# Embedding stage of a one-block vision transformer: loads, scales and all four engine queues in a new order

## The reference

```python
xn = x * rsqrt(mean(x * x, -1) + 1e-6)                       # per patch
scale = 127.0 / clip(max(abs(xn), -1), 1e-5)
xq = clip(round(xn * scale), -128, 127) / scale
ws = 1.0 / clip(mean(abs(w)), 1e-5)
wq = clip(round(w * ws), -1, 1) / ws
h = concatenate([cls, xq @ wq.T], 1) + pos
# attention on layernorm(h)
num = exp(q_rot @ k_rot.T * dh ** -0.5)
den = sum(exp(q @ k.T * dh ** -0.5), -1)                     # without rotation, without mask
h = h + where(causal, num / den, 0) @ v @ Wout + bout
h = h + expert_attention(layernorm(h))
```

## Time and profile before

| what | before |
|---|---|
| median of 3 runs | 259.35 us (258.7 to 259.77) |
| the profiled execution | 258.43 us, span 256.6 us |
| busy in the span | PE 219.7, DVE 181.8, ACT 101.5, POOL 71.3 us |
| instructions | PE 2047, DVE 316, ACT 200, POOL 69 |
| mean granted clock of TensorE | 0.96 |

### The profile page before, as it was taken

The page is one execution under the profiler, slowest core; times in us unless marked ns, Lnnn a source line. Parts: engine busy times, 40 slices in busy tenths (PEclk is TensorE's granted clock), DMA queues, the critical chain, the costliest instruction groups (busy, mean ns, idle before and its releaser), DMA issues.

```text
span 256.6 us, 5086 instructions
## 1 busy us (share of the span) xinstructions
PE 219.7 (86%) x2047; PEld 194.0 (76%) x2047; DVE 181.8 (71%) x316; ACT 101.5 (40%) x200; POOL 71.3 (28%) x69
## 2 busy tenths in 40 slices
PE   0317475999987787999999999999999999999995
PEld 0206374999966555999777788787899999999994
DVE  1598798865379977584244564856679997979982
ACT  3567543885677312657534016425520211120000
POOL 0103648900035020100051555595666000000000
PEclk9999757799999997999999999999999999999999
DMA  7993000000002000000061200704702452461102
GB/s 242 295 411 125 0 1 3 1 0 3 0 3 87 3 3 0 1 3 0 0 187 72 82 3 1 245 3 127 228 3 52 168 155 77 142 213 47 51 0 96
DMA packets 7037, 20.08 MB, mean 78 GB/s; under 512 B 1027, under 2 KB 1606, under 8 KB 6758
## 3 DMA queue, kind: packets, MB, share of 16 engines
q1 hardware_dynamic: 7014, 19.76, 23.7%
HBM read 19.07 MB, written 0.68 MB: 77 GB/s over the span
## 4 chain that ended last, share of the span: by engine, by line
PE 58%; DVE 26%; issue 7%; DMA 3%; ACT 2%; POOL 1%; SPq 1%; DVEq 0%
PE ps L263 15%; PE ps L264 14%; PE ps L265 14%; DVE gx L1073 7%; DVE xhat L807 4%; PE ps L1373 3%; DMA vrow<-vectors 3%; DVE rden L905 2%; PE ps L1248 2%; PE ps L1403 2%; DVE oelo L1047 2%; DVE stat L796 2%; PE ps L1205 2%; DVE en L888 1%; PE ps L1121 1%
## 5 line engine op out<-in xcount | busy, mean ns | idle before, releaser
L1011 DVE COPY_PREDICATED v<-onehot,ps 128x512 f32<-128x512 uint8 (+3 forms) x40 | 26.2, 660 | 24.1 <-PE ps L265 23.9
L1073 DVE TENSOR_TENSOR gx<-maskb,oT 128x1184 fp32r<-128x1184 bf16 x31 | 42.3, 1408 | 0.6 <-PE ps L265 0.5
L263 PE MATMUL ps<-gx,oelo 128*128 128x296 f32 x124 | 37.8, 305 | 0.6 <-DVE gx L1073 0.6
L265 PE MATMUL ps<-gx,oehi 128*128 128x296 f32 x124 | 37.2, 300 | 0.0
L264 PE MATMUL ps<-gx,oehi 128*128 128x296 f32 x124 | 37.0, 298 | 0.0
L263 PE MATMUL ps<-vehi,x2lo 128*128 128x512 f32 (+3 forms) x90 | 35.1, 390 | 0.0
L264 PE MATMUL ps<-velo,x2hi 128*128 128x512 f32 (+3 forms) x90 | 33.3, 370 | 0.0
L265 PE MATMUL ps<-vehi,x2hi 128*128 128x512 f32 (+3 forms) x90 | 33.1, 368 | 0.0
L446 POOL TENSOR_TENSOR velo<-veraw,vehi 128x1024 fp32r<-128x1024 f32 x8 | 19.2, 2404 | 49.2 <-ACT vehi L626 49.1
L263 PEld LDWEIGHTS ps<-gx,oelo 128*128 128x128 f32 x124 | 23.3, 188 | 1.8 <-issue 1.3
L264 PEld LDWEIGHTS ps<-gx,oehi 128*128 128x128 f32 x124 | 23.4, 189 | 0.0
(11 more groups left out here) (162 smaller groups left out, 521.1 us busy)
## 6 DMA issues: line engine op xcount, KB each, us to landing
maskb<-mask_rows SPq DMA_DIRECT2D x32, 148.0 KB, 3.7
veraw<-value_w SPq DMA_DIRECT2D x8, 512.0 KB, 3.9
oeraw<-output_w SPq DMA_DIRECT2D x8, 512.0 KB, 3.6
xp<-x_rows SPq DMA_DIRECT2D x6, 336.0 KB, 6.8
wqraw<-w_qkv SPq DMA_DIRECT2D x1, 1280.0 KB, 11.3
w2raw<-w_qkgate SPq DMA_DIRECT2D x1, 1088.0 KB, 13.3
tw<-tok_weight SPq DMA_DIRECT2D x1, 768.0 KB, 5.0
out<-yo SPq DMA_DIRECT2D x4, 148.0 KB, 1.9
```

The source lines that it names most:

```text
L263: pe.matmul(o, llo, rhi, start=start, stop=False)
L265: return pe.matmul(o, lhi, rhi, start=False, stop=stop)
L1011: dve.copy_predicated(v2[0:m, t, h0:h1], bcast(onehot[0:m, t, h0:h1, e], 2, DH2), ps[0:m, JBANK[n], 0:(h1 - h0) * DH2].rearrange("p (a b) ...
L1073: dve.tensor_tensor(gx[:, k % NGR].rearrange("p a b t -> p a (b t)"), bcast(maskb[:, w % NMR, k % MEU], 1, 2), oT[:, c % 2].bitcast(F32), ...
```

## The change

- **Loads (SP).** The order was x0, weight, x1, x2, constants, vectors, x3, x4, x5. It becomes x0, the identity part of the constants, x1, weight, x2, x3, the other constants, vectors, x4, x5; then as before.
- **Scales per group.** `msq` and its power go to GpSimd, group by group; `quant_scales` takes a list of groups ([0], [1], [2], [3], [4, 5]), multiplies and clamps in one step, and `dqs` is made once for all groups.
- **qT.** All six copies out of PSUM are on ScalarE, and `qT` has four buffers and not two.
- **Queues.** Groups 0 and 1 are quantised before the ternary weight is made; TensorE's start follows a written list, `START`. Four projection jobs stand in it.
- **PSUM banks of the projections** are given out in another order, so that jobs 2 to 5 don't wait for the last `x1_lo`.
- **GpSimd.** `gate_sel` is made early. `qkv_lo(g)` waits until `xhat` of group g is written. The bias additions to `h` come before `w2_lo`, and wait for the last `x1_lo`. The four `w2_lo` wait for the attention's `den_ps` 1, 1, 2 and 3. `ve_lo(0)` waits for the third `x2_lo`, `ve_lo(1)` for the last.
- `w2raw` lies in another part of SBUF, which lives until the end of the attention.

```diff
@@ block.sync
-            sp.dma_start(xp[:, 0, :], x[0]).then_inc(x_in[0], 16)
+            x_load(0)
+            sp.dma_start(cst[:, 0:P], consts[:, 0:P]).then_inc(ident_in, 16)
+            x_load(1)
             sp.dma_start(tw[:], tokw).then_inc(tokw_in, 16)
-            for g in range(1, GI):
-                sp.dma_start(xp[:, g, :], x[g]).then_inc(x_in[g], 16)
-            sp.dma_start(cst[:], consts).then_inc(const_in, 16)
+            x_load(2)
+            x_load(3)
+            sp.dma_start(cst[:, P:], consts[:, P:]).then_inc(const_in, 16)
             sp.dma_start(vrow[:], vecs).then_inc(vec_in, 16)
-            for g in range(GI, G):
-                sp.dma_start(xp[:, g, :], x[g]).then_inc(x_in[g], 16)
+            x_load(4)
+            x_load(5)
@@ banks and TensorE's start
-        PJB = [6, 7, 4, 5] + [0, 1, 2, 3] + [4, 5, 6, 7] + [0, 1, 2, 3] + [4, 5, 6, 7] + [4, 5, 6, 7]
+        PJB = [6, 7, 0, 1] + [2, 3, 4, 5] + [6, 7, 0, 1] + [2, 3, 4, 5] + [6, 7, 0, 1] + [6, 7, 4, 5]
+        START = [("turn", 0), ("turn", 1), ("total", 0), ("bias", 0), ("turn", 2), ("embed", 0), ("turn", 3), ("embed", 1),
+                 ("turn", 4), ("embed", 2), ("turn", 5), ("x", 0), ("embed", 3), ("x", 1), ("embed", 4), ("x", 2),
+                 ("embed", 5), ("x", 3), ("job", 0), ("x", 4), ("job", 1), ("x", 5), ("job", 2), ("job", 3)]
@@ block.gpsimd
-            for b in range(2):
-                pool.wait_ge(sm["msq_ready"], b + 1)
-                s_ = slice(GI * b, GI * b + GI)
-                pool.tensor_tensor(rrms[:, s_], msq[:, s_], half_neg[0:R, :], ALU.pow).then_inc(sm["rrms_ready"], 1)
+            for g in range(G):
+                pool.wait_ge(sm["sq_done"], g + 1)
+                s_ = slice(g, g + 1)
+                pool.tensor_scalar(msq[:, s_], ssq[:, s_], 1.0 / DIN, 1e-6, ALU.mult, ALU.add).then_inc(sm["msq_ready"], 1)
+                pool.wait_ge(sm["msq_ready"], g + 1)
+                pool.tensor_tensor(rrms[:, s_], msq[:, s_], half_neg[0:R, 0:1], ALU.pow).then_inc(sm["rrms_ready"], 1)
+            pool.wait_ge(const_in, 16)
+            pool.tensor_copy(gate_sel[:], bcast(cols("hsel", NH2 * NE), 2, DH2)).then_inc(sm["pool_setup"], 1)
...
-            for g in range(G):
-                pool.wait_ge(sm["lnv_ready"], g + 1)
-                pool.tensor_tensor(rstd[:, 0, g:g + 1], ...)
-                if g < 5:
-                    qkv_lo(g)
+            rstd_of(0, 0)
+            rstd_of(0, 1)
+            for g in range(G - 1):
+                pool.wait_ge(sm["xhat_ready"], g + 1 if g + 2 < G else G)
+                qkv_lo(g)
+                if g + 2 < G:
+                    rstd_of(0, g + 2)
+            pool.wait_ge(sm["x1lo_ready"], G)
+            for g in range(G):
+                pool.tensor_tensor(h[:, g], h[:, g], biasb[:, 1], ALU.add).then_inc(sm["h0b_ready"], 1)
             for n in range(4):
+                pool.wait_ge(sm["den_ps"], max(n - 1, 0) + 1)
                 w2_lo(n)
-            for g in range(G):
-                pool.wait_ge(sm["xhat_ready"], g + 1)
-                pool.tensor_tensor(h[:, g], h[:, g], biasb[:, 1], ALU.add).then_inc(sm["h0b_ready"], 1)
-            for e in range(NVR):
-                ve_lo(e)
+            for g in range(GI):
+                rstd_of(1, g)
+            pool.wait_ge(sm["x2lo_ready"], GI)
+            ve_lo(0)
+            for g in range(GI, G):
+                rstd_of(1, g)
+            pool.wait_ge(sm["x2lo_ready"], G)
+            ve_lo(1)
@@ block.scalar, the start
+            square(0)
+            round_up(0)
+            square(1)
+            quantised_T(0)
+            round_up(1)
+            square(2)
+            square(3)
+            quantised_T(1)
+            square(4)
             act.wait_ge(sm["tern_pre"], 1)
             act.activation(tern[:], tw[:], ACT.Copy, bias=-ROUND).then_inc(sm["tern_ready"], 1)
+            round_up(2)
+            square(5)
+            bias_rows()
+            quantised_T(2)
+            round_up(3)
+            round_up(4)
+            quantised_T(3)
+            round_up(5)
+            wq_hi(0)
+            quantised_T(4)
+            wq_hi(1)
+            quantised_T(5)
+            x1_hi(0)
...
@@ block.vector, the start
+            absmax(0)
+            dve.wait_ge(ident_in, 16)
+            dve.tensor_copy(ident_bf[:], cols("ident")).then_inc(sm["ident_ready"], 1)
+            quant_scales([0])
+            absmax(1)
+            quantised(0)
+            quant_scales([1])
+            dve.wait_ge(tokw_in, 16)
+            dve.tensor_reduce(small[:, 0:1], tw[:], AX, ALU.add, apply_absolute_value=True).then_inc(sm["wabs"], 1)
+            quantised(1)
+            dve.wait_ge(sm["tot_ps"], 1)
...
+            absmax(2)
+            quant_scales([2])
+            absmax(3)
+            quant_scales([3])
+            quantised(2)
...
+            absmax(4)
+            absmax(5)
+            quant_scales([4, 5])
+            dve.tensor_scalar(dqs[:], amc[:], small[0:R, 3:4], None, ALU.mult).then_inc(sm["dqs_ready"], 1)
+            quantised(3)
             embed(0)
-            quantised(3)
+            quantised(4)
             embed(1)
+            quantised(5)
             ln_apply(0, 0)
-            quantised(4)
             embed(2)
             ln_apply(0, 1)
             x1_lo(0)
-            quantised(5)
```

181 lines of the change are left out of this document (75 added, 106 removed).

## The result

| what | before | after |
|---|---|---|
| median, measured together | 259.56 us (258.7 to 260.23) | 248.5 us (247.98 to 249.89) |
| ratio, 95% interval | | 0.960 (0.957 to 0.964) |
| the profiled execution | 258.43 us, span 256.6 | 248.44 us, span 246.6 |
| first matmul of the scores | 69.91 us | 59.07 us |
| first residual addition | 90.66 us | 79.79 us |

A forecast was written before the change was run, and what follows sets the result against it. It took VectorE's chain to bound the kernel, with 6.7 us of held layer norm applications in the embedding. Its terms, -5.8 (job 2 earlier), -1.15 (clock) and -0.1 (attention), made -7.05 from 259.35: 252.3 us, range 250.4 to 255.8.

The forecast's parts named there:

- E: Rival, embedding: every application from the second on is held by wqlo and the power, 261.9 us; chance 0.04.
- F: Rival, projections: rope or ScalarE's reads hold them and hide the gain, only 1 us left, 258.3 us; chance 0.05.
- The clock's term: Start of the projections: TensorE at 2.4 GHz gives back 1.65 us, job 8's wait takes 0.5, net 1.15.
- The attention: Moved w2lo and velo change the holds on mask multiplies: -0.4 to +0.2 us, taken as -0.1.
- A: Main case, embedding to attention: the sum of the terms, -7.05 us, 252.3 us; chance 0.42.
- C: Rival, attention: a pair of w2lo holds the mask multiply for both, 254.4 us; chance 0.18.
- B: Rival, start of the projections: the clock is low again there, 253.4 us; chance 0.18.
- job 2 at 39.6: End of the embedding: TensorE begins the dense projections at 39.6 and not 45.4, 5.8 us earlier.
- The front: Embedding up to embed(0): new small GpSimd steps and waits put embed(0) at 23.95, 1.1 us later than before.
- The rounds: Embedding, one group to the next: 2.1 us on VectorE, 2.1 to 2.3 with TensorE at 1.2 GHz.
- The tail: Embedding's end: embed(5) at 35.3, then TensorE's x3, job 0, x4, job 1, x5; x1_lo(5) ends at 40.4.
- rival D: Embedding: the clock is high there too, VectorE alone paces it, job 2 at 38.2, 250.9 us; chance 0.13.

The follow-up runs named there:

- e3: The kernel before with useless matmuls in TensorE's idle stretches between 26 and 45 us, to keep the clock high; ratio 0.997 (0.993 to 1.001).
- e2: The changed kernel with GpSimd's order of before, all else as changed; 255.35 us, ratio 0.987.
- e8: The changed kernel with the four w2lo still in the attention, but behind the masks of a batch; 246.61 us, ratio 0.952.
- e6: The changed kernel with the four w2lo put behind the last small power, beside the last layer norm application; 252.25 us, ratio 0.972.
- e15: The changed kernel with the transposes of groups 3, 4 and 5 ahead of all four projection jobs, second run; 251.44 us, ratio 0.971.
- e11: The changed kernel with the banks of the projection jobs given out as in the kernel before; 249.99 us, ratio 0.962.
- e14: The kernel before with GpSimd's new order, and VectorE's quantised for group 5 moved ahead of the second application; 249.67 us, ratio 0.967.
- e5: The kernel before with GpSimd's new order alone, run again for another profile; 248.8 to 252.7 us, no interval.
- e1: The kernel before with GpSimd's new order alone, first run; 249.3 us, ratio 0.962.
- e9: The kernel before with GpSimd's new order, and useless matmuls on TensorE before the fifth and sixth groups' transposes; 252.73 us, ratio 0.970.
- e7: The changed kernel with the four w2lo released earlier, when VectorE has finished the third set's rotation and idles; 247.15 us, ratio 0.954.

## Why the prediction was wrong

**Right.** The sign, and the mechanism of the largest term: the three holds are gone, and the `wqlo` between two applications meets the embed (of which only the first instruction reads PSUM). E and F fell with it: no application above 0.42 us, and TensorE busy without a hole in the 3.4 us behind the start of job 2 and still from 44 to 60 (16.0 of 16 us). The clock's term was right: the projections are 23.26 us long from job 2 to the scores (59.07 - 35.81) against 24.53 before (69.91 - 45.38), 1.27 us less where I had 1.65 - 0.5 = 1.15. In e3, where job 8 waits for nothing, they are 22.98 (68.39 - 45.41): the clock gives 1.55, and job 8's wait takes 0.26 and not 0.5. The attention: forecast -0.1, measured 20.72 against 20.75. The mask multiply took 1.91 (forecast 1.8 in A, 3 in C), so a pair of `w2lo` holds it for one of them only, and C fell; B fell by the clock of 1.00 at job 2.

**Wrong: job 2 at 39.6.** It came at 35.81, 3.79 us ahead of that. The step that failed is the working of the embedding, from the front to the last low part of x1: x1_lo(5) ended at 36.86 and not at 40.4, 3.54 us, in three pieces; the last 0.25 is that job 2 begins 1.05 us ahead of that end and not 0.8.
1. *The front, 1.07 us.* "A `tensor_scalar` of one column on GpSimd [...] I take 0.4", and 0.65 for the power. They took 0.19 and 0.56 for the two groups on the path: 0.30 less each time. Half of my bound from nothing to 0.86 was too much for an operation on one column. The weight's sum began at 10.07 and not 10.55, `tern` ended 0.7 earlier, and the steps behind it ran closer together by another 0.4.
2. *The rounds, 1.36 us.* "A round on VectorE is 1.27 + 0.41 + 0.40 = 2.1 us; with TensorE at 1.2 GHz [...] 2.1 to 2.3". Embed(5) was forecast 11.35 us behind embed(0) and came 9.99 behind it (32.87 - 22.88). Some 0.8 us of it is the addition of durations. Of two instructions in a row the next starts up to 0.1 us ahead of the end that its predecessor's row gives: the application at 30.34 lasts 0.41, and the next instruction starts at 30.67. 2.08 added up is 1.90 from start to start. The other 0.57 is what I allowed TensorE at 1.2 GHz between the first application and embed(3) (28.45 to 31.1 for 2.08 of VectorE's work). The clock had risen by then: that group's product took 0.82. And at 1.2 GHz the allowance would have been too much: e2 has one round of 2.11 and the next at 1.90. A round of 1.90, from 37.19 to 39.09, stood in the trace that I predicted from.
3. *The tail, 1.11 us.* From embed(5) to the end of x1_lo(5) I had 5.1 us, by TensorE at 1.2 GHz in turn x3, job 0, x4, job 1, x5; it took 3.99. Here TensorE does set the pace. In the trace of e8, which has the same embedding, the clock stood at 0.63 from 32 to 36 us, embed(0) was 0.24 us earlier and x1_lo(5) ended 0.67 later: by that pair of traces some 0.9 of the 1.1 is clock.

So rival D, a high clock through the embedding, came true from 28 us on, with the 0.13 that I gave it, but explains only the last piece and a part of the second; D itself said 38.2 for job 2, because it inherited the other errors. My argument against it, "at 2.4 GHz TensorE has gaps there", was true of the gaps (0.85 and 0.83 us ahead of two transposes) and false of the clock here: it stayed at 1.00 across them. That was in part luck. In e8 and e6, with two gaps of 0.83 us in the same places, it fell (0.63 and 0.65 from 32 to 36 us); in e15, where a gap of 1.49 us follows, it fell to 0.82.

**The rest of the difference.** 3.79 us of job 2 and 0.12 of the projections make 3.9 at the scores; the median came out 3.8 below the forecast. Between the two profiled executions it is 2.9, since 0.9 us was lost behind the residual addition, which the forecast had at nothing.

**Where the 10.84 us at the scores come from.** Undone one at a time in the changed kernel: GpSimd's order 6.7 (e2), jobs in TensorE's gaps 2.3 (e15), banks 0.95 (e11). These add up to 9.9, if they may be added; the 0.9 left would be the front's, which was not undone alone. Each comes from one pair of traces, and kernels with this same front have embed(0) anywhere from 22.56 to 22.98, so a few tenths of each are not the edit's. What the new front does is seen from the other side: with the old one a `quantised` takes the application's place beside `wqlo` (1.5 us for 0.55; about 1 us at the scores by e14), and the weight's load is waited for. By single edits to the kernel before, GpSimd's order was worth 7.9 (e5) where the loads came as in its trace. Of the spread over 4 to 5 us with the old front (e1, e5, e9) the load is a part by three traces, the clock by two; I have not separated them.

**What the ports did.** VectorE's application beside three `w2lo` in a row took 4.01 and 4.00 us over 3.92 in e2 and e6, as before (and 4.04 in e3). The rule of the Trainium skill ("SBUF — State Buffer", Who interferes with whom), by which a holder blocks for its own length, is at odds with these traces. For the mask multiply it is borne out: two `w2lo` from 65.63, and it waited for one. What tells the two cases apart was not tried; the application has one tensor input, the multiply two. The multiply seems to hold in turn: of those two `w2lo` the first took 1.42 us and the second, which it runs beside, 1.87, where they take 1.31 on average in a row of three.

## What to carry to other kernels

Put the second engine's subtractions where the first reads PSUM, and check each instruction that an edit moves next to them. Here the hold moved from the application to `quantised`, while the layer norm's statistics, also read from SBUF, were never held. When an order is written by hand, read a round's length from start to start in the trace, never as a sum of durations. Put work that TensorE has anyway into its gaps: here two jobs were worth their own length (1.7 us) and 0.7 of clock behind them. And read the granted clock over the whole span ahead of any talk of causes: the largest difference between e8 and the changed kernel was a stretch at 1.2 GHz, more than 10 us behind the last instruction that the edit moves.

## What I had not expected of the hardware

- Three GpSimd subtractions in a row (3.92 us) hold VectorE's application until the last has ended, in four kernels; beside two of them (3.25 us) a multiply with two tensor inputs gets in after the first (1.91 us for 0.76).
- The granted clock differs between executions of the same work: 1.00 from 32 to 36 us in the changed kernel (twice), in e7 and in e11, 0.63 in e8 and 0.65 in e6. In e8 its price up to the scores was 0.7 us, 0.9 counted from embed(0). From 88 to 92 us it was 0.50, 0.61, 0.66 or 1.00, and cost up to 1.8 us.
- The column of the granted clock prints 1.00 also where the trace has no record of the clock. In the changed kernel it is 1.00 from 20 us on, but its first record is at 28.4 us: six products take 1.49 us, as at 1.2 GHz, until the one at 25.4, then 1.07 at 27.9 and 0.82 from 29.1. The first record is at 24.9 us in the trace of before and at 34.2 in e2. Ahead of it the duration of a known instruction is the witness.
- A power of one column on GpSimd takes 0.55 to 0.82 us, a multiply and addition of one column 0.19; the power that ran beside VectorE's clip of the weight took 1.95.
